# The states' layer: experts one state ahead, VectorE's parts one state behind, softplus at the eleventh state, and the first sequence normalized in front of other moments

## Time and profile before

| what | us |
|---|---|
| median of 3 runs | 1861.52 |
| profiled execution, its own time | 1864.82 |
| its span, first to last instruction | 1863.0 |
| PE busy | 1535.0 (82%) |
| DVE (VectorE) busy | 1146.8 (62%) |
| ACT busy | 1058.3 (57%) |
| POOL busy | 209.6 (11%) |
| first state starts on VectorE | 45.5 |
| last state ends on VectorE | 467.7 |

### The profile page before, as it was taken

One profiled execution on the slowest core, in us unless ns is written; L12 is line 12 of the kernel. 1 busy time (PEld: TensorE's weight loads), 2 busy tenths in 40 slices (PEclk: granted clock), 3 DMA queues, 4 the chain that ended last, 5 costly groups with the idle time before them and its releaser, 6 DMA issues. The chain is left out here.

```text
span 1863.0 us, 24105 instructions
## 1 busy us (share of the span) xinstructions
PE 1535.0 (82%) x8656; PEld 780.7 (42%) x8656; DVE 1146.8 (62%) x2283; ACT 1058.3 (57%) x1786; POOL 209.6 (11%) x152
## 2 busy tenths in 40 slices
PE   5999999988699688976889868898677788877785
PEld 2555556555345344432444424443233242322352
DVE  4789989999764853456543565433535676664522
ACT  4788778776124147643466434666465535775685
POOL 1333342432000000000000000000000000001003
PEclk9999999999799789887898878988577777995998
DMA  4423232353301120112000221000450322030002
GB/s 160 132 69 80 74 87 69 89 147 96 108 19 52 41 63 18 32 54 77 27 18 22 64 66 38 18 18 1 111 136 1 103 104 78 17 91 27 14 3 74
DMA packets 91623, 116.32 MB, mean 62 GB/s; under 512 B 10096, under 2 KB 71536, under 8 KB 91120
## 3 DMA queue, kind: packets, MB, share of 16 engines
q1 hardware_dynamic: 89808, 110.05, 21.1%
q0 software_dynamic: 1696, 4.72, 0.9%
HBM read 83.27 MB, written 31.46 MB: 62 GB/s over the span
## 5 line engine op out<-in xcount | busy, mean ns | idle before, releaser
L1682 ACT ACTIVATE scratch<-ps 128x1024 f32<-128x1024 f32 x288 | 287.0, 1021 | 191.6 <-PE ps L1307 70.4
L2114 DVE TENSOR_REDUCE neg_max<-ps 128x2 f32<-128x1024 f32 (+2 forms) x224 | 233.1, 1067 | 113.6 <-PE ps L1252 112.7
L1671 ACT ACTIVATE ps<-ps 128x512 f32<-128x512 f32 x256 | 150.1, 586 | 97.6 <-PE ps L1297 97.1
L1331 PE MATMUL ps<-scratch,values 128*32 128x512 f32 (+3 forms) x1344 | 177.5, 616 | 14.8 <-ACT scratch L1682 9.3
L1970 DVE TENSOR_TENSOR_SCAN scratch<-scratch 128x512 f32<-128x512 f32 x128 | 159.5, 1285 | 2.7 <-ACT scratch L1642 2.4
L1878 DVE SCALAR_TENSOR_TENSOR gated<-tanh,ps 128x512 f32<-128x512 f32 x88 | 60.4, 686 | 139.8 <-ACT tanh L1570 139.6
L1570 ACT ACTIVATE tanh<-ps 128x512 f32<-128x512 f32 x88 | 52.3, 594 | 163.5 <-PE ps L1024 163.3
L1059 PE MATMUL ps<-xnt,weights_even 128*128 128x512 f32 x256 | 125.8, 613 | 7.4 <-ACT gated L1553 6.6
L2294 POOL TENSOR_SCALAR variance_eps<-mean_var 128x4 f32<-128x4 f32 x20 | 5.3, 263 | 1006.6 <-DVE mean_var L1798 1006.6
L1024 PE MATMUL ps<-xnt,weights_odd 128*128 128x512 f32 x176 | 113.1, 729 | 0.0
L1027 PE MATMUL ps<-xnt,weights_odd 128*128 128x512 f32 x176 | 99.8, 651 | 7.2 <-DVE values L2096 7.2
(11 more groups left out here) (328 smaller groups left out, 2859.5 us busy)
## 6 DMA issues: line engine op xcount, KB each, us to landing
scratch<-state_rows SPq DMA_DIRECT2D x64, 512.0 KB, 4.8
scratch<-parts_scratch SPq DMA_DIRECT2D x288, 96.0 KB, 2.4
parts_scratch<-weights_even SPq DMA_DIRECT2D x168, 128.0 KB, 2.4
weights_odd<-in_l SPq DMA_DIRECT2D x8, 519.5 KB, 6.5
weights_even<-in_l SPq DMA_DIRECT2D x1, 4096.0 KB, 15.6
weights_odd<-in_l SPq DMA_DIRECT2D x1, 4096.0 KB, 13.9
parts_scratch<-gated SPq DMA_DIRECT2D x15, 128.0 KB, 2.4
slots_scratch<-head_out SPq DMA_DIRECT2D x5, 256.0 KB, 5.3
```

Source lines behind the costliest of these rows:

```text
L1331: mm = pe.matmul(ps[32 * i:32 * i + 32, PV, q0:q0 + n], (vx[b % 2] if l == 3 else vx[l - 1])[:, c, VW * h:VW * h + 32], grain(l, b, s)[:, ...
L1671: ins = act.activation(bank, bank, ACT.Exp, accum_out=dens[:, j, h:h + 1])
L1682: act.activation(dst, src, ACT.Exp).then_inc(q[l, "exp_done"], 1)
L2114: ins = dve.tensor_reduce(dst, ps[:, base:base + 2, col:col + n], AX.X, ALU.max, negate=True)
```

## The change

`HEAD0_AT` and `TAIL0_AT` place the head of the next sequence and the tail of the one before by the state after which they stand. In `first_layer` the experts' step after state n is f of n+2 instead of n+1, with two f steps in front of the first state; scaling `sc` and adding `ac` move one state forward with them. On VectorE three parts get a name and place of their own, behind the engine's step that they wait for: `gd` (its part of `gate`), `mc` (of `mb0`), `ob` (of `op`); for the first `q` of layer 1 it is `qs`. `xv` stands one state later, beside `zs`; `hl` stands after state 11 instead of 12, and `ge` after 9 instead of 8. The last state is moved behind the last experts and the projections of queries and keys. `causal_alone` puts the first two `f` of layer 1 in front of `nm` and `tr` of the last sequence. The banks of the up matmuls rotate in another order. At the start xn of sequence 0 is made in front of the moments of sequence 1.

```diff
 HEAD0_AT = {0: (("hx", 0),), 1: (("hx", 1),), 2: (("hx", 2),), 3: (("hx", 3),), 4: (("cv", 0), ("hz", 0)), 5: (("cv", 1),),
-            6: (("xv", 0),), 7: (("gate", 0), ("zs", 0)), 8: (("ge", 0), ("dt", 0)), 9: (("dt", 1), ("cw", 0)),
-            10: (("br", 0), ("mb0", 0)), 12: (("hl", 0),), 13: (("ds", 0),)}
-TAIL0_AT = {0: ("yg",), 1: ("op",), 3: ("cb",), 5: ("nm",), 6: ("tr",)}
-HEAD0_FIRST = [("hx", c) for c in range(4)] + [("cv", 0), ("cv", 1), ("gate", 0), ("hz", 0), ("xv", 0), ("zs", 0),
+            7: (("gate", 0), ("xv", 0), ("zs", 0)), 8: (("gd", 0), ("dt", 0)), 9: (("ge", 0), ("dt", 1)),
+            10: (("cw", 0), ("br", 0)), 11: (("mb0", 0), ("hl", 0)), 12: (("mc", 0),), 13: (("ds", 0),)}
+TAIL0_AT = {0: ("yg",), 1: ("op",), 2: ("ob",), 3: ("cb",), 5: ("nm",), 6: ("tr",)}
+HEAD0_FIRST = [("hx", c) for c in range(4)] + [("cv", 0), ("cv", 1), ("gate", 0), ("gd", 0), ("hz", 0), ("f", 0), ("xv", 0), ("zs", 0),
                ("dt", 0), ("dt", 1), ("br", 0), ("ge", 0), ("hl", 0), ("cw", 0), ("ds", 0)]
...
-    out += [("da", 0, 0, 0), ("f", 0, 0, 0)]
+    out += [("da", 0, 0, 0), ("f", 0, 0, 1)]
     for b in range(NB):
         for s in range(NST):
             n = NST * b + s
+            if n == STATES - 1:
+                out += [("fl", 0, b, STATES), ("ac", 0, b, EXPERTS - 2), follow[0], ("sc", 0, b, EXPERTS - 1),
+                        ("ac", 0, b, EXPERTS - 1), follow[1]]
             out.append(("s", 0, b, n))
             if n == 0:
-                out += [("mb0", 0, 0, 0), ("mb1", 0, 0, 0)]
-            if s % 2 == 0 and n:
-                out.append(("sc", 0, (n // 2 - 1) // E0, n // 2 - 1))
-            out.append(("f" if n + 1 < STATES else "fl", 0, (n + 1) // NST, n + 1))
+                out.append(("mb0", 0, 0, 0))
+            if n == 1:
+                out.append(("mc", 0, 0, 0))
+            if n == 2:
+                out.append(("mb1", 0, 0, 0))
+            if s % 2 == 1 and n + 1 < STATES:
+                out.append(("sc", 0, (n // 2) // E0, n // 2))
+            if n + 2 < STATES:
+                out.append(("f", 0, (n + 2) // NST, n + 2))
             if s % 2 == 0 and n + 2 < STATES:
                 out.append(("da", 0, (n + 2) // NST, n + 2))
             if b:
                 out += [(what, 0, b - 1, 0) for what in TAIL0_AT.get(s, ())]
             if b and s == 4:
                 out += [("mb1", 0, b, 0), ("ac", 0, b, n // 2 - 2)]
-            elif s % 2 == 1 and n > 1 and (s != 3 or not b):
+            if s % 2 == 0 and n and (s != 2 or not b) and n + 2 < STATES:
                 out.append(("ac", 0, (n // 2 - 1) // E0, n // 2 - 1))
...
-    out += [follow[0], ("sc", 0, b, EXPERTS - 1), ("ac", 0, b, EXPERTS - 1), follow[1], ("tg", 0, b, 0), ("yg", 0, b, 0), ("op", 0, b, 0)]
-    out += follow[2:3] + [("cb", 0, b, 0)] + follow[3:4]
-    out += [("nm", 0, b, 0), ("tr", 0, b, 0)]
-    return out + follow[4:]
+    out += [("tg", 0, b, 0), ("qs", 1, 0, 0), ("yg", 0, b, 0), ("op", 0, b, 0), ("qs", 1, 0, 1)]
+    return out + [("ob", 0, b, 0), follow[2], ("cb", 0, b, 0)] + follow[3:]
...
-    out = weave(a, chunks(0, 0, 7)) + [("mx", 1, 0, 0)] + chunks(0, 7, 9)
+    units = weave(a, chunks(0, 0, 7))
+    early = [item for item in units if item[0] == "f"][:2]
+    units = [item for item in units if item not in early]
+    out = early + [("nm", 0, NB - 1, 0)] + units[:4] + [("tr", 0, NB - 1, 0)] + units[4:] + [("mx", 1, 0, 0)] + chunks(0, 7, 9)
...
-            return (1, 2, UP)[f % 3] if l == 0 else UP
+            return (UP, 2, 1)[f % 3] if l == 0 else UP
...
                             pe.wait_ge(s_experts, 16)
+                            pe.wait_ge(q[0, "head_seen"], 3)
+                            pe.wait_ge(xnt_ready[before[l]], NB + 1)
+                        if n == 1:
                             pe.wait_ge(q[0, "head_seen"], HEAD0_USES)
-                            pe.wait_ge(xnt_ready[before[l]], NB + 1)
...
             first_moments(0)
+            first_normed(0)
             first_moments(1)
-            first_normed(0)
             constants0()
```

7 lines of the change are left out of this document (4 added, 3 removed).

## The result

The changed kernel takes 1851.01 us (median of 5 runs, 1849.13 to 1852.24), the kernel before 1861.52 (5 runs, 1860.2 to 1867.56): ratio 0.993, 95% interval 0.9906 to 0.9953. It is faster, by less than 1%, and the 10.5 us between the medians are half of what was forecast. The time lies inside the range, but outside the forecast's own spread of 1833 to 1848: the likeliest case was not what happened.

A forecast was written before the change was run, and what follows sets the result against it. VectorE was taken to set the pace, PE close behind. Terms −2.9 −8 −6 −1.2 −4 = −22.1 gave 1842.7 us for a profiled run, 1840 for the median; range 1827 to 1857.

The forecast's parts named there:

- rival D: States' layer: ACT's scaling behind the decays holds the expert bank, PE stops at every odd state; 1878 us, chance 0.07.
- rival B: States' layer: PE or ACT takes over as the bound; first and middle sequences −2 each, total 1853 us, chance 0.18.
- Head: Before the first state: earlier xn −1.0, dt at full pace −3.2, one more table load +1.3; together 2.9 us sooner.
- First sequence: First sequence's states: most waits go, 3.5 of xconv's 8.9 us stay, five additions become paid; −8 us.
- Middle sequences: Two middle sequences: waits of 7.7 and 8.8 us go, five additions become paid in each; −1.5 and −4.5 us.
- moves on queues: States' layer: ACT's scaling behind the decays is just hidden from PE, which waits 1.2 us once a sequence; costed at nothing.
- VectorE's parts: All sequences: parts moved to where inputs are a state old remove VectorE's waits; −8, −6 and −1.2 us.
- Paid additions: States' layer: POOL's additions, no longer hosted in removed waits, lengthen VectorE's products by 1.07 or 0.86 us each.
- Table loads: ACT: 13 more, four in each of three sequences and one in the head, hidden beside VectorE's 104 us.
- Last sequence: Last sequence: one branch wait of 2.3 us goes, less one addition; −1.2 us.
- Passage: Passage into the next layer: branch 1.8 us sooner, values and first two f chunks fill VectorE's wait; −4 us.
- rival C: Passage: whoever comes sooner waits there for PE or the stacks, so −22 shrinks to −7.5; 1854 us, chance 0.08.

The follow-up runs named there:

- after_pool_small: Changed kernel with GpSimd's addition to the second running sum on 16 columns instead of 512; 1840.92 us, ratio 0.9888.
- lead0_sp10: Changed kernel with the experts' old cadence (lead0) and softplus one state earlier, behind the decays of state 10; 1825.85 us, ratio 0.9787.
- head_f0_back: Changed kernel with the experts' first up-product back behind the head instead of between the first sequence's projections; 1849.51 us, ratio 0.9929.
- lead0: Changed kernel with the experts' old cadence: up-products one state ahead, scaling at even states ahead of the decays; 1830.19 us, ratio 0.9808.
- lead0_parts_back: lead0 with VectorE's parts, softplus, the gate's exponential and the mixtures' steps back at their old states; 1857.64 us, ratio 0.9965.
- lead0_mix_back: lead0 with only the first mixture's three steps back together, between the first state and the next up-product; 1838.95 us, ratio 0.985.
- lead0_sp10_ge10: lead0_sp10 with the gate's exponential also a state later, behind the same decays and ahead of softplus; 1827.54 us, ratio 0.9795.
- loads: Changed kernel with the gate's exponential one state later, behind that state's decays, and its followers a state or two later; 1851.49 us, ratio 0.993.
- experts_only: Kernel before with only the change's expert cadence (up-products two states ahead, scaling behind the decays) and banks' order; 1872.14 us, ratio 1.0063.
- softplus_small: Changed kernel with softplus's three activations on 16 columns instead of 512, the logarithm replaced by an exponential; 1833.83 us, ratio 0.983.
- sc_first: Changed kernel with each scaling moved to the even state before, ahead of the decays, experts still one ahead; 1839.37 us, ratio 0.9865.

## Why the prediction was right, and where not

**The number.** 1851 lies in the range because the range is wide and because two errors of opposite sign met, as is shown below; that part is luck. Up to the end of the changed stretch the profile has 7.3 us of the 22.1. Of the signs that the prediction named, these came: dt's 8 passes (3.68 us), xconv's wait in the first sequence (3.8), the end of the branch (9.0 us after the last state), the table loads (14 for 13). These did not: VectorE's waits at the four named lines are 12.0 us in the layer and not under 5, the middle sequences take 109.3 us and not 103 to 106, and VectorE is busy 100.6 and 97.5 of them and not 102. Both signs of being wrong that fit are there: PE waits for queries_keys (D), and VectorE's waits for PE stay (B). So for the middle sequences the mechanism was wrong although the time lies in the range.

**What bounds the layer: half wrong.** I took VectorE for the pace and put PE's work at 96 us. In the last sequence VectorE is the bound. In the middle ones of the changed kernel PE is busy 102 us, and after_pool_small shows them deaf to 8 to 11 us of VectorE's work. My 96 left out the lower clock after stops; 97.1 and 100.7 busy, in lead0_sp10 where the clock was 1.00, is what PE shows without it, and the rest of the difference was not traced.

**Head, −2.9: right.** −2.45, and dt's 8 passes ran in 3.68. But head_f0_back shows that of the 3.0 us of the first up-product little arrives: it flows into PE's stop right after. The order of the moments was not tested by itself.

**First sequence, −8: −6.0.** xconv's wait of 3.8 us (3.5 was worked out) and PE's stop of 8.0 (some 8) are where they were put. But 2.2 of the gate's 3.3 stayed, decays are waited for 3.5 us instead of 2.4, and PE stands 6.2 us for the scaling, which the forecast had at nothing.

**Middle sequences, −6: +3.8.** The step that failed is *moves on queues*, "I cost it at nothing, ends 0 and +3.6". It was computed from PE's even state to the scaling with gelus, decays and loads between, and came out "just hidden". It left out softplus, which the change puts in front of these, and set the stop of 1.2 us that it did find at nothing. Measured is the cadence's price, 21 us at the medians against lead0. The profile has 7.6 of it in the first sequence, 5.3 and 4.7 in the middle ones and 1.5 in the last, and 1.1 come back in head and passage. It is the mechanism of rival D at a smaller size, with rival B's time: 22.2 us of stops in 17 places, one of them 4.35 in each of three sequences, and the lower clock behind it. Rival D's ground against it, "the middle period of 6.7 us leaves more than 1 us of slack", holds for a typical state and not for the one with softplus.

**VectorE's parts, −15.2 over all sequences: undersized in the first, about right elsewhere.** With the old cadence, so without the cadence's stops, lead0 is shorter than the kernel before by 13.5 in the first sequence (for −8, and beyond that term's end of −13), 3.7 and 2.4 in the middle ones (6.1 for −6), and 1.7 in the last (for −1.2). lead0_parts_back gives 23.4 us in the profile and 27 at the medians. In the first sequence I had let PE keep much of its lag; 7.6 us of it hang on its 10 us stop (lead0_mix_back). This error and that of *moves on queues* have opposite signs, which is why the total fell inside the range.

**Paid additions: right in kind, priced too high.** An addition costs 0.68 us in the last sequence by after_pool_small, below my 0.86 to 1.07. Where the waits did go, in lead0, VectorE's busy time in the middle sequences rose by 2.5 and 1.9 us, not by 5.3 and 4.3. In the changed kernel it rose by 1.5 and 0.4, and nobody waits for VectorE there. The rule of the Trainium skill, SBUF — State Buffer, "Who interferes with whom", agrees in kind: with the additions on 16 columns VectorE is busy 8 to 11 us less in a middle sequence.

**Table loads: 14 for 13, hidden or not by place.** The six fewer of lead0_sp10_ge10 and the twelve fewer of loads bring nothing (in both VectorE waits for the gate's exponential in their place, 4.7 and 8.3 us, so these runs do not show a load alone to be free); two a sequence fewer and a better place in lead0_sp10 remove a 3.5 us stop. Each is 1.283 us and the next activation follows at once (load at 235.59, activation at 236.89).

**Last sequence, −1.2: −0.3** (yg to last scan, 89.3 to 89.05). **Passage, −4: −2.4.** The times that I gave for it after the last state came within 1 us up to the first two chunks; what I missed is the wait for PE behind them, rival C's mechanism at 2.4 us.

**Behind the passage nothing was changed**, and yet the medians of lead0 differ from before by 33 us where the profile has 25 up to there, those of lead0_parts_back by 7 where it has 1, those of experts_only by +9 where it has +14. Each of them gains 5 to 8 us later (the changed kernel 3 at the medians, 8 in the profile). From the fourth maximum to the end the profiled executions take 1325 to 1330 us in eleven of the fourteen kernels, but 1336.0 in the kernel before, 1332.4 in experts_only and 1341.9 in softplus_small. So 8.4 us of the profiled pair's 15.7 lie in one long rest of the kernel before. At the medians 3 us of the 10.5 are left, nearly a third of the gain, and their cause stays open.

## What to carry to other kernels

Where two engines are both busy over 90% of a period, take neither as the bound from busy time: shrink one's work and see whether the period moves, and then the other's. When a step is moved to run further ahead, look for what frees the buffer it needs next, and add up everything that stands in front of that release on its engine in the fullest period, not in the typical one; work with slack (softplus, decays) belongs behind such a release. And a change of many edits is worth splitting: this one held −27 and +21 us, both measured from `lead0` by the medians.

## What the hardware showed that I had not expected

- A stop of PE can cost more than its length. With 3.16 us of idling in front of them dt's 8 passes took 6.65 us at a granted clock of 0.55, with 1.34 us they took 3.68 at 1.00. After the 4.34 us stop the granted clock was 0.52 for some 5 us, and 0.97 over the middle sequences; in lead0_sp10, without these stops, it was 1.00.
- Taking away twelve table loads of 1.283 us won nothing (loads), while ACT's work in front of the scaling costs more than the stop it makes: softplus_small took away 3.7 us of PE's stops a middle sequence and won 5.1 and 7.2 us.
- A stop is the remainder of a sum: 3.84 us of ACT's work taken from in front of the scaling (sc_first) made a stop of 4.34 us one of 0.49.
- Executions of one kernel spread differently: 1824.22 to 1831.17 in 5 of lead0, 1836.31 to 1858.88 in 12 of head_f0_back. I read differences under 0.5% from landmarks, each from one execution.
